# A two-layer decoder block on one NeuronCore: row scores of the cross attentions in four row strips, and an explicit activation table preload behind each SiLU of the mamba loop

## The reference

```
x = x + L0_attn(layernorm(x))     # two mambas (forward and backward), d_inner 512, 16 states
x = x + L0_xattn(layernorm(x), ctx, ctx)   # 16 heads of 16, 64 keys, "causal" mask tril(1024 x 64)
x = x + L0_ffn(layernorm(x))      # self attention block and a mixture of 8 experts, top 2
x = x + L1_attn(layernorm(x))     # one mamba
x = x + L1_xattn(layernorm(x), ctx, ctx, padding_mask)
x = x + L1_ffn(layernorm(x))      # three coupling cycles
```

## Time and profile before

| | |
|---|---|
| time of three runs | 2925.09 us median, 2921.03 to 2925.59 |
| the profiled execution: first to last instruction | 2927.1 us, mean granted TensorE clock 0.944 |
| busy: PE, DVE, ACT, POOL | 2456.1, 1872.1, 1332.9, 1530.9 us |
| mambas of layer 0, about | 41 to 1044 us of the span |
| cross attention x0, from its first row scores to its last matmul | 1062.2 to about 1160.5 us |
| mamba of layer 1, about | 2155 to 2659 us |
| cross attention x1, from its first row scores on | 2677.9 to about 2790.5 us |
| table loads in the loops of the mambas, 1.283 us each | L764 26, L716 12, L704 10, L749 8, L754 8, L738 4 |

### The profile page before, as it was taken

How to read it: one execution, slowest core, us unless ns; L and a number is a source line. 1 busy time by engine, 2 the same in 40 slices (tenths; PEclk the granted TensorE clock), 3 DMA queues, 4 the chain that set the end, 5 groups by cost and what they waited for, 6 DMA issues and landing times. The chain is left out here.

```text
span 2927.1 us, 26112 instructions
## 1 busy us (share of the span) xinstructions
PE 2456.1 (84%) x8044; PEld 1106.1 (38%) x8044; DVE 1872.1 (64%) x2521; ACT 1332.9 (46%) x2087; POOL 1530.9 (52%) x1340
## 2 busy tenths in 40 slices
PE   7989989889897788688888549999588989778978
PEld 3333323333332233333333338888332333223322
DVE  2999999999999933466663400000239999994334
ACT  4656466565664433345555212222056565542333
POOL 2999999999999811500000230000439999982010
PEclk9999999999999999899999669999689999999989
DMA  4031230321203000612310324444230320300000
GB/s 186 1 115 47 94 117 1 122 70 55 115 1 115 0 21 17 141 24 33 45 23 1 138 106 181 177 175 175 79 155 1 116 94 24 115 1 20 0 9 29
DMA packets 72193, 215.12 MB, mean 73 GB/s; under 512 B 14044, under 2 KB 39271, under 8 KB 53495
## 3 DMA queue, kind: packets, MB, share of 16 engines
q1 hardware_dynamic: 65380, 180.85, 18.9%
q10 hardware_dynamic: 3602, 24.22, 2.5%
q0 software_dynamic: 3072, 8.39, 0.9%
HBM read 187.80 MB, written 25.43 MB: 73 GB/s over the span
## 5 line engine op out<-in xcount | busy, mean ns | idle before, releaser
L895 POOL TENSOR_TENSOR s_dbu<-s_dx,s_bc 128x512 f32<-128x512 f32 x768 | 967.8, 1284 | 47.9 <-DVE s_psum L561 44.1
L480 PE MATMUL s_psum<-s_hc,ident 128*128 128x512 f32 x1536 | 832.2, 632 | 181.2 <-DVE s_hc L581 170.2
L764 ACT ACTIVATE s_psum<-s_dt,s_a_neg 128x512 f32<-128x512 f32 x768 | 521.6, 688 | 590.5 <-DVE s_hc L581 589.5
L480 PEld LDWEIGHTS s_psum<-s_hc,ident 128*128 128x128 f32 x1536 | 257.9, 192 | 695.2 <-DVE s_hc L581 505.4
L581 DVE TENSOR_TENSOR s_hc<-s_psum,s_bc 128x512 f32<-128x512 f32 x624 | 419.8, 673 | 0.6 <-PE s_psum L480 0.4
L561 DVE TENSOR_TENSOR_SCAN s_psum<-s_psum,s_state,s_dbu 128x512 f32<-128x512 f32 x312 | 395.1, 1277 | 18.5 <-ACT s_psum L764 12.7
L561 DVE TENSOR_TENSOR_SCAN s_psum<-s_psum,s_dbu 128x512 f32<-128x512 f32 x312 | 381.3, 1222 | 22.0 <-ACT s_psum L764 13.8
L1968 ACT ACTIVATE s_probs<-s_banks 128x512 f32<-128x512 f32 (+3 forms) x384 | 169.2, 493 | 149.5 <-PE s_banks L1693 107.0
L2381 POOL DMA_INDIRECT s_rows_in<-moe_out_rows,s_place x32 | 30.6, 957 | 357.0 <-DMA moe_out_rows<-s_ys 347.5
L2360 ACT ACTIVATE s_hidden<-s_banks,s_w 128x256 f32<-128x256 f32 x184 | 77.1, 470 | 300.9 <-PE s_banks L2183 300.9
L163 POOL TENSOR_TENSOR s_pair<-s_res 128x512 f32<-128x512 f32 x4 | 5.0, 1265 | 386.1 <-issue 384.6
(11 more groups left out here) (306 smaller groups left out, 3320.6 us busy)
## 6 DMA issues: line engine op xcount, KB each, us to landing
s_bc<-fwd_rows SPq DMA_DIRECT2D x64, 1024.0 KB, 4.7
s_bc<-m_rows SPq DMA_DIRECT2D x32, 1024.0 KB, 4.7
s_w<-in_moe_w SPq DMA_DIRECT2D x23, 1028.0 KB, 7.2
s_w<-in_moe_w ACTq DMA_DIRECT2D x23, 1024.0 KB, 5.5
qk_parts<-s_parts SPq DMA_DIRECT2D x48, 128.0 KB, 1.9
s_stack_q<-qk_parts SPq DMA_DIRECT2D x48, 128.0 KB, 4.5
s_stack_k<-qk_parts SPq DMA_DIRECT2D x48, 128.0 KB, 7.6
moe_in_rows<-s_zero SPq DMA_DIRECT2D x1, 5888.0 KB, 18.8
```

The lines of the kernel that those rows point to most:

```text
L480: pe.matmul(psum[:, SCANS + block_no % 2, :], consts["ident"][:], hc[:, unit % PRODUCTS, :], start=(n == 0), stop=(n == NS - 1)).then_inc( ...
L764: act.activation(psum[:, unit % SCANS, :], dt[:, g % 2, i // NS, :], ACT.Exp, scale=a_neg[CHUNKS[g][0]][:, i:i + 1]).then_inc(decay_ready, 1)
L895: pool.tensor_tensor(dbu[:, unit % TERMS, :], dx[:, g % 2, i // NS, :], bc[:, 2 * n, :], ALU.mult)\
```

## The change

The cross attentions' `rows` is called for two tiles at a time, and makes the scores in four strips: strip r uses partitions 32r to 32r+31 of q and `kd`, and the 2 heads of each feature half that lie there, so 128 columns. Strip r writes its own bank, SC + r. That is 16 float32 matmuls of 32 x 128 against 128 columns for a pair of tiles in place of four of 128 x 128 against 512. The key mask is added in four strips of three rows, one matmul for each bank and pair; the causal mask with four full matmuls of 256 columns for a pair. `maskb` and `ones3` get 128 partitions, and SyncE fills the mask's strips with 12 small DMAs instead of 3. As a pair fills all four banks, the second pair waits for the maxima of the first. `maxima` reads a tile's scores across four banks, so the order of heads in the maxima changes, and `pick` with it. `project(c + 1)` moves between the two pairs, and `out(c - 1)` from behind `shift(c, 0)` to before `turn(c)`. `center` moves behind the last maxima, `store_q` before `square_of`, `pair_square` behind the last spread.

In the mambas two lines are added: behind `silu_u` and behind `silu_gate` ScalarE preloads the set that holds both exp and ln.

```diff
@@ mixers, scalar
                     if g + 1 < NC and i == 22:
                         silu_u(g + 1)
+                        act.preload_act_table_set("natural_log_exp_and_others")
@@
                     if i == 55:
                         silu_gate(g)
+                        act.preload_act_table_set("natural_log_exp_and_others")
@@ cross_attention, sync
-                for part in range(3):
-                    sp.dma_start(maskb[part:part + 1, :, :], mask_parts[:, part, :]).then_inc(mask_stored, 16)
+                for r in range(HH):
+                    for part in range(3):
+                        sp.dma_start(maskb[r * VW + part:r * VW + part + 1, :, :], mask_parts[:, part, :])\
+                          .then_inc(mask_stored, 16)
@@ tensor
+            def rows(c, p):
+                b = c // BCH
+                if p == 0:
+                    pe.wait_ge(q_stored, KD * (c + 1))
...
+                        pe.wait_ge(probs_ready, 4 * c)
+                else:
+                    pe.wait_ge(maxed, TILES * c + 2)
+                late_here = causal and c % BCH == 0 and p == 0
+                for t in range(2):
+                    n = c * TILES + 2 * p + t
+                    for hb in range(KD):
+                        for r in range(HH):
+                            mm = pe.matmul(banks[:, SC + r, (KD * t + hb) * P:(KD * t + hb + 1) * P],
+                                           q[r * VW:(r + 1) * VW, hb, n * P:(n + 1) * P],
+                                           kd[r * VW:(r + 1) * VW, b, hb, 2 * r:2 * r + 2, :],
...
+                if late_here:
+                    pe.wait_ge(mask_ready, 1)
+                    for r in range(HH):
+                        mm = pe.matmul(banks[:, SC + r, 0:KD * P], consts["identb"][:],
+                                       late[:, 0:SK].unsqueeze(1).to_broadcast([P, 2 * KD, SK]),
                                        start=False, stop=True)
...
+                    for r in range(HH):
+                        mm = pe.matmul(banks[:, SC + r, :], ones3[r * VW:r * VW + 3, :],
+                                       maskb[r * VW:r * VW + 3, b, :].unsqueeze(1).to_broadcast([3, 4 * KD, SK]),
@@ shift
+                if k == 0:
+                    pe.wait_ge(maxed, TILES * (c + 1))
@@ the loop
                 rows(c, 0)
+                if c + 1 < NCH:
+                    project(c + 1)
                 rows(c, 1)
                 if c + 2 < NCH:
                     mean(c + 2)
-                rows(c, 2)
-                rows(c, 3)
-                if c + 1 < NCH:
-                    project(c + 1)
+                if c:
+                    out(c - 1)
                 turn(c)
                 shift(c, 0)
-                if c:
-                    out(c - 1)
@@ vector, maxima
-                u = SC + 2 * (i % 2)
-                dve.tensor_reduce(nmax[:, i % 2, :], banks[:, u:u + 2, :].rearrange("p c (h s) -> p (c h) s", s=SK),
+                cs = slice(i % 2 * KD * P, (i % 2 + 1) * KD * P)
+                dve.tensor_reduce(nmax[:, i % 2, :].rearrange("p (r h) -> p r h", r=HH),
+                                  banks[:, SC:SC + HH, cs].rearrange("p r (h s) -> p r h s", s=SK),
```

More of the change, by code:

```diff
@@ L987, in cross_attention @@
             mask_parts = s.sb("mask_parts", [1, 3, B * SK], BF16)
-            maskb = s.sb("maskb", [3, B, SK], BF16)
-            ones3 = s.sb("ones3", [3, P], BF16)
+            maskb = s.sb("maskb", [P, B, SK], BF16)
+            ones3 = s.sb("ones3", [P, P], BF16)
         k_loaded, v_loaded, q_loaded, o_loaded = (s.sem("k_loaded"), s.sem("v_loaded"), s.sem("q_loaded"),
@@ L1097, in project @@
                     mm.then_inc(q_ready, 1)
-            def rows(c, i):
-                b, n = c // BCH, c * TILES + i
-                if i == 0:
+            def rows(c, p):
+                b = c // BCH
+                if p == 0:
                     pe.wait_ge(q_stored, KD * (c + 1))
[L1103 to L1118, removed]
-                                       start=False, stop=True)
[L1120 to L1124, removed]
@@ new lines, in rows @@
+                    if c == 0:
+                        pe.wait_ge(kd_ready, B * KD)
+                        pe.wait_ge(k_stored, KD)
+                        pe.wait_ge(vd_ready, B)
+                    else:
+                        pe.wait_ge(probs_ready, 4 * c)
+                else:
+                    pe.wait_ge(maxed, TILES * c + 2)
[7 more added lines that the diff above has]
+                                           kd[r * VW:(r + 1) * VW, b, hb, 2 * r:2 * r + 2, :],
+                                           start=(t == 0 and hb == 0),
+                                           stop=causal and not late_here and t == 1 and hb == KD - 1)
@@ new lines, in rows @@
+                if late_here:
[3 more added lines that the diff above has]
+                                       late[:, 0:SK].unsqueeze(1).to_broadcast([P, 2 * KD, SK]),
+                                       start=False, stop=True)
+                if not causal:
+                    if c == 0 and p == 0:
+                        pe.wait_ge(mask_stored, 3 * HH * 16)
+                        pe.wait_ge(made, 3)
+                    for r in range(HH):
+                        mm = pe.matmul(banks[:, SC + r, :], ones3[r * VW:r * VW + 3, :],
+                                       maskb[r * VW:r * VW + 3, b, :].unsqueeze(1).to_broadcast([3, 4 * KD, SK]),
@@ L1140, in shift @@
                 b = c // BCH
+                if k == 0:
+                    pe.wait_ge(maxed, TILES * (c + 1))
                 for r in range(HH):
[L1142 to L1145, removed]
+                    if k and r % 2 == 0:
                         pe.wait_ge(probs_ready, 4 * c + r // 2 + 1)
@@ L1308, in _ @@
                     divide(c - 1, 1)
+                maxima(c, 2)
+                maxima(c, 3)
                 if c + 2 < NCH:
                     center(c + 2)
-                maxima(c, 2)
-                maxima(c, 3)
                 if c:
@@ L1394, in _ @@
             for c in range(NCH):
+                if c + 1 < NCH:
+                    store_q(c + 1)
                 if c + 2 < NCH:
                     square_of(c + 2)
-                if c + 1 < NCH:
-                    store_q(c + 1)
                 store_nmax(c)
@@ L1440, in _ @@
                 spread_max(c, 1)
+                spread_max(c, 2)
+                spread_max(c, 3)
                 if c + 2 < NCH:
                     pair_square(c + 2)
-                spread_max(c, 2)
-                spread_max(c, 3)
                 if c + 3 < NCH:
@@ L2680, in layout @@
     a["key_cols"] = np.tile(i["mask_Bx1x1xS2_ff0"].reshape(B, SK).T, (2, 1))
-    head = 8 * np.arange(KD)[None, :, None] + 2 * (part // 32)[:, None, None] + (part // SK)[None, None, :]
+    head = 4 * (part // 32)[:, None, None] + KD * np.arange(KD)[None, :, None] + (part // SK)[None, None, :]
     a["pick"] = (part[:, None, None] % 32 == head).astype(np.float32)
```

2 lines of the change are left out of this document (1 added, 1 removed).

## The result

The changed kernel takes 2875.11 us, the median of four runs (2872.07 to 2878.81); the kernel before took 2924.97 beside it (2921.03 to 2925.59). The ratio is 0.9833 with a 95% interval of 0.982 to 0.9846: 45 to 53 us less. The forecast was 2875. The two traces span 2870.4 and 2927.1 us.

A forecast was written before the change was run, and what follows sets the result against it. PE's streaming bounds the cross attentions; DVE, with GpSimd close behind, the mambas. Cross attentions win 36.7 us (x0 11.2, x1 25.5), tables 13.6, together 50.3: 2925.1 to 2875 us. Range of 8 in 10: 2861 to 2891.

The forecast's parts named there:

- A pair of tiles at 0.96 us: Cross attentions' row scores: four strips side by side, weight loads hidden, take 0.96 us a pair against 3.43 before.
- groups of 16 that start 0.21 us apart: Sign in PE's timeline: the new rows' line has 256 records in each stage, in groups of 16 starting 0.21 us apart.
- The change of form: PE in the cross attentions: going between strips and full matmuls costs 0.2 us, two to three more times a chunk.
- its last tail: Last chunk of each cross attention, from the last pick on: 10.8 to 8.8 us, 2.0 won in each.
- the head of x1's chunk 3: Second cross attention, last chunk, first row scores to first `pick`: 14.2 to 10.2 us, 4.0 won.
- Rivals A and B: Cross attentions' strips: A, loads not hidden, pair 1.8 us, total 2885, chance 0.13; B, strips serial, 2915, chance 0.04.
- the wait of `turn` in chunk 0: First chunk of x0: without `out` to cover it, `turn` waits for GpSimd's copy until 9.0 us into the head.
- Tables: Mambas: preloads behind each SiLU remove ScalarE's other table loads; 13.6 us won together, bounds 8.5 and 26.
- the 2.05 for one chunk: Layer 0's second to seventh chunk: 2.05 us each of DVE's 2.49 stall goes, bounds 1.2 and 2.49; 12.3 together.
- over 0.4 us a chunk held by the terms: Sign against the tables' part: it would be wrong if GpSimd's terms hold DVE by more than 0.4 us a chunk.
- the bare load: Behind layer 0's last mamba chunk one ScalarE table load is bare; removing it wins 1.28 us.
- Rival E: Cross attentions: PE less busy, so its granted clock could fall to 1.2 GHz; half the chunks 2943, all 3011; chance 0.04.

## Why the prediction was right, by its own steps

**Strips.** A pair of tiles at 0.96 us: right. Its first record stands 0.21 us ahead of the next and the others follow 0.11 apart in each strip, four strips side by side, as priced; only the sign "groups of 16 that start 0.21 us apart" was put wrongly. The change of form, taken as 0.2 us, was 0.14 in one of its two rows (1.00 less 0.86) and 0.20 in the other; it is 0.15 behind a pair now. From first rows to first pick and from pick to pick, x0 won 9.3 us where the sum had 9.2, and its last tail, from the last pick to the last `out`, 2.0 (12.8 to 10.8) as forecast. x1 won 22.1 where it had 23.5, and 2.0 in its last tail. The one term off by more than 0.3 us is the head of x1's chunk 3, 11.8 us and not 10.2: that is the fall of the clock. Rivals A and B, a bare load or serial strips, are out: each would show in every pair.

**Waits moved.** There is no wait before the second pair but in chunk 3; the wait of `turn` in chunk 0 is 1.7 us, and that for the exponentials 1.1 in chunks 2 and 3, all as worked out. What the order of PE is worth in all, I did not ask in the prediction, and put too low later: 21 us by the medians, of the 33 that the strips and the order give, 15.5 of them waits.

**Tables.** From the first scan of the second chunk to that of the eighth it was 719.3 us (185.10 to 904.42) and is 706.9: six chunks won 12.4 us, forecast 12.3. They won 1.85 and 2.27 by turns, between the bounds of 1.2 and 2.49. So the sum is right, but the 2.05 for one chunk was a choice between the bounds, and by its own sign (over 0.4 us a chunk held by the terms) every other chunk, with 0.64, is on the wrong side. The last chunk with its tail won 3.4, not 1.28: the bare load as forecast, 0.56 of a wait for a decay in the last chunk that I had passed over, and 1.5 of clock. Layer 1's chunks won 0.14 each, forecast 0; behind its last chunk 1.7 us were lost, by output matmuls that took 8.80 us and not 7.11, at a lower clock. 15 us measured alone against 13.6.

**No drain behind a load.** The Trainium skill (ScalarE: Activation LUTs, What ACT_TABLE_LOAD costs) has a drain of about a load's length behind each switch. The last rows of ScalarE above show an activation 1.30 us after the start of its load, and no run here shows a drain behind one.

**Rival E** was the right mechanism, at a place where I had not priced it. I weighed whole loops at half clock, and held against it that the waits of before are of 1 to 2 us; but the sum itself had made a wait of 2.5 us in chunk 3. I read the granted clock in the 3 us behind each of PE's waits in the cross attentions' loops, in thirteen traces (all but that with four term buffers). Behind 33 waits of 2.4 to 3.1 us it was below 1.00 in 28; behind 19 of 2.2, ahead of the last `out`, in 4; behind 18 of 1.6 to 1.7, in 4. Behind the 14 waits of 1.6 us or more that a fill had covered, it was below 1.00 in none. So the waits bring the fall, but not each time and not at each place: x0's wait of 2.48 us leaves the clock at 1.00 in both traces of the changed kernel, while in three variants with the same wait in the same program of PE it is 0.52 to 0.74 behind it. Why, no run here settles. In the changed kernel's trace this costs 1.6 us, in that of the old order 8 more, in that with one preload 8 more too. The prediction held because one such wait is left in each stage, and in part by luck: in two variants with the same program of PE the clock cost 4 and 8 us more.

**Sum.** 36.7 + 13.6 = 50.3 forecast; 33 + 15 measured alone, 49 together. That it meets the forecast to a us is partly luck: in the traces x1's loop gave 1.4 us too little and layer 1's end lost 1.7, while layer 0's last chunk with its tail gave 2.1 more than forecast and layer 1's chunks 0.4. (The prediction's "2.0 above the median" sets a trace's span against device times; the changed kernel's trace spans 1.9 us less than the device time of the same execution. The sum doesn't use it.)

## What to carry to other kernels

Here a matmul with 16 of 128 contraction rows in use took 0.86 us like a full one. Strips side by side gave that back, in proportion to the columns that each strip streams (1.11 us a pair of tiles with 128, 1.93 with 256, 3.43 with full matmuls), and neighbours of one form saved the 0.1 to 0.2 us of the change between them. Once PE is no longer full, look at its order too, which held 21 of the 33 us here: put the long independent matmuls where the result of another engine is awaited. A wait of 2.4 us or more was mostly paid a second time, by a lower clock behind it (28 of 33). As that share differs between variants whose TensorE program is the same, don't credit it to an edit from one trace: compare the idle time, and the busy time of the same matmuls, apart. When a stall of one engine goes, read what its neighbour had gained from it, idle time above all, and expect the rest of the stall back as a wait for that neighbour.

## What was not expected of the hardware

Behind a wait of 2.45 us in the old order TensorE's granted clock stood at 0.50 for several us: 32 records of row scores took 2.09 us instead of 1.17, a `project` 5.92 instead of 3.60. Unread matmuls in a wait of 2.78 us kept it at 1.00. A matmul only 3 rows deep between full ones cost changes of form as a strip does: 0.3 us for each of 32 banks of x1, gone when it was padded with zeros to 128 rows, though that streams as many columns.
